# Head sums on VectorE, routing one slot earlier, and a last attention unit laid out for the experts

## The reference

```python
xn = layernorm(x)
# branch 1: linear attention, 16 heads of 32, chunks of 128, decay per head
q, k, v = silu(xn @ Wq), silu(xn @ Wk), silu(xn @ Wv)
scores  = (q @ k.T) * D                      # within a chunk
o       = scores @ v + (q @ S) * q_decay     # S: state before the chunk
S       = exp(ld * 128) * S + (k * k_decay).T @ v
o  = o * sigmoid((xn @ Wg1) @ Wg2)
o  = o * rsqrt(mean(o * o over the head's 32) + 1e-5) * norm_w
a  = o @ Wo
# branch 2: 8 experts, best 2 per token, at most 1280 slots an expert, in order of tokens
p, e = top2(softmax(xn @ Wg))
m  = sum over 2 of p * (relu(xn @ w1[e]) @ w2[e])     # 512 -> 2048 -> 512
return x + a + m
```

## Time and profile before

| what | us |
|---|---|
| median of 3 runs (2173.14 to 2176.17) | 2175.56 |
| the profiled execution | 2182.53 |
| its span, first to last instruction | 2180.8 |
| TensorE busy | 2110.3 |
| VectorE busy | 765.1 |
| ScalarE busy | 573.5 |
| GpSimd busy | 477.6 |
| mean granted TensorE clock | 0.988 of full |

### The profile page before, as it was taken

The page is one execution under the profiler, slowest core; times in us unless marked ns, Lnnn a source line. Parts: engine busy times, 40 slices in busy tenths (PEclk is TensorE's granted clock), DMA queues, the critical chain, the costliest instruction groups (busy, mean ns, idle before and its releaser), DMA issues.

```text
span 2180.8 us, 28220 instructions
## 1 busy us (share of the span) xinstructions
PE 2110.3 (97%) x11672; PEld 1741.4 (80%) x11672; DVE 765.1 (35%) x1486; ACT 573.5 (26%) x1017; POOL 477.6 (22%) x372
## 2 busy tenths in 40 slices
PE   6899999999979999999999999999999999999997
PEld 4787788778768888878887887888888888878886
DVE  5555565555454113312422322331232124223311
ACT  5222322332233212312312321231232123113211
POOL 2524442443350111020211202101010202111011
PEclk9899999999989999999999999999999999999998
DMA  4220212011025122321622413332141215224021
GB/s 151 77 78 31 70 60 78 21 60 60 32 68 198 26 49 67 118 44 44 159 28 62 111 60 68 74 111 30 52 113 59 40 49 144 42 55 112 28 30 20
DMA packets 83964, 151.39 MB, mean 69 GB/s; under 512 B 16768, under 2 KB 16768, under 8 KB 83824
## 3 DMA queue, kind: packets, MB, share of 16 engines
q1 hardware_dynamic: 63424, 105.65, 14.6%
q0 software_dynamic: 20400, 43.74, 11.4%
HBM read 109.82 MB, written 39.53 MB: 68 GB/s over the span
## 4 chain that ended last, share of the span: by engine, by line
PE 86%; DMA 5%; DVE 3%; issue 2%; POOL 2%; ACT 1%; SPq 0%; POOLq 0%; ACTq 0%; DVEq 0%
PE bank L1074 43%; PE bank L1349 29%; PE bank L1211 4%; DMA out_rows<-y,add_row 4%; PE bank L1081 3%; PE bank L1387 2%; POOL out_rows L564 1%; PE bank L1158 1%; DMA gathered<-xn_rows,gather_row 1%; PE bank L1175 1%; PE bank L1200 1%; DVE xnT_lo L801 1%; PE bank L1122 1%; PE bank L1194 1%; PE bank L1168 0%
## 5 line engine op out<-in xcount | busy, mean ns | idle before, releaser
L1026 DVE SCALAR_TENSOR_TENSOR h_lo<-bank,h_hi 128x512 fp32r<-128x512 f32 x256 | 177.1, 692 | 788.2 <-ACT h_hi L741 788.2
L1074 PE MATMUL bank<-xT_hi,w_hi 128*128 128x512 f32 x1024 | 406.6, 397 | 0.5 <-issue 0.5
L1074 PE MATMUL bank<-xT_hi,w_lo 128*128 128x512 f32 x1024 | 399.6, 390 | 0.0
L1349 PE MATMUL bank<-w_hi,h_lo 128*128 128x512 f32 x1024 | 398.6, 389 | 0.0
L1074 PE MATMUL bank<-xT_lo,w_hi 128*128 128x512 f32 x1024 | 398.5, 389 | 0.0
L1349 PE MATMUL bank<-w_hi,h_hi 128*128 128x512 f32 x1024 | 398.3, 389 | 0.0
L1349 PE MATMUL bank<-w_lo,h_hi 128*128 128x512 f32 x1024 | 398.3, 389 | 0.0
L741 ACT ACTIVATE h_hi<-bank 128x512 fp32r<-128x512 f32 x256 | 153.1, 598 | 823.5 <-PE bank L1074 823.5
L564 POOL DMA_INDIRECT out_rows<-y,add_row x80 | 128.8, 1611 | 777.0 <-ACT y L734 704.9
L1074 PEld LDWEIGHTS bank<-xT_hi,w_lo 128*128 128x128 f32 x1024 | 192.2, 188 | 41.6
L1349 PEld LDWEIGHTS bank<-w_lo,h_hi 128*128 128x128 f32 x1024 | 192.2, 188 | 39.9
(11 more groups left out here) (185 smaller groups left out, 2434.8 us busy)
## 6 DMA issues: line engine op xcount, KB each, us to landing
raw_weights<-in_L_ffn_w SPq DMA_DIRECT2D x256, 256.0 KB, 4.1
x_in<-in_L_attn_x SPq DMA_DIRECT2D x32, 256.0 KB, 3.2
xn_rows<-xn SPq DMA_DIRECT2D x32, 256.0 KB, 2.2
x_res<-in_L_attn_x SPq DMA_DIRECT2D x32, 256.0 KB, 4.6
out_rows<-y_attn SPq DMA_DIRECT2D x32, 256.0 KB, 2.0
gathered<-xn_rows,gather_row POOLq DMA_INDIRECT x80, 3.5
out_rows<-y,add_row POOLq DMA_INDIRECT x80, 5.1
attn_raw<-in_L_attn_Wq SPq DMA_DIRECT2D x4, 256.0 KB, 7.8
```

Of the source, the lines that this page charges most:

```text
L1026: v_.scalar_tensor_tensor(h_lo[f % 2][:, 0:n * P], h_bank[f % 2][:, 0:n * P], 0.0, h_hi[f % 2][:, 0:n * P].bitcast(F32), ALU.max, ALU.subt ...
L1074: last = mm(dest, at(left[l], t), at_r(right[r], t), start=(i == 0), stop=(i == n - 1))
L1349: last = mm(y_bank[i][:, :], hx[f % 2][:, part], wx[c][:, f % FPC, :], start=(f == 0 and l == 0), stop=(f == FT - 1 and l == 2))
```

## The change

**Head sums and scales.** gate_output is followed by a VectorE transposition of gated in blocks of 32x32, into a new tile turned: a head's 32 rows become 32 neighbouring columns. ScalarE squares turned, VectorE reduces over 32 columns (sum_sq), adds eps, GpSimd takes the power, VectorE multiplies turned by the scales, read with a repeated column, and transposes the product back into normed. sum_squares, turn_scales, spread_scales, head_cols and the bank for scales are gone. xn is turned into sc[0], sc[1] and the two banks of q and k.

**Routing.** turn_logits follows the four v projections, read_logits and choose follow the fourth unit's normalise (for the first group, they stand ahead of the first unit), count and read_counts are at i = 0, give_slots between that unit's masks and states, the eight route DMAs at i = 0, with the second norm_scale behind them.

**The last unit and memory.** raw lies elsewhere, so the first eight weight units are loaded at unit 28 and four are split there, four in unit 30; gather_rows(0) is in unit 29. The first four gathers are issued in unit 30, into the expert's tile y. The last unit is written out for TensorE: parts of the group's out projection stand between its steps, and the rest (finish_out) behind the first up of expert 0. Up now waits for a chunk's first four weight units only, down for all eight.

**Between experts.** The confirm of the last spare moves behind the first two gathers of the next expert.

Declarations and places of tiles, and those changes of counts that follow from the rest, are left out:

```diff
...
+                    if g == SUPERS - 1:
+
+                        sp.wait_ge(S["xn_turned"], TILES)
+                        for s in xn_stored:
+                            sp.wait_ge(s, 16 * SUPERS)
+                        for n in range(UNITS):
+                            load_unit(0, n)
                     if g > 0:
                         for j in range(TPG):
                             store_y(TPG * (g - 1) + j)
+                    if g == SUPERS - 1:
+                        sp.wait_ge(S["routed"], 16 * TOP * TILES)
+                        sp.dma_start(slot_rec[:, main_cols, :], main_slots[0]).then_inc(S["rec_loaded"], 16)
+                        sp.dma_start(slot_rec[:, spare_cols, :], spare_slots[0]).then_inc(S["rec_loaded"], 16)
...
+            def first_gathers():
+
+                pool.wait_ge(S["gather_rows_ready"], 1)
+                for s in xn_stored:
...
+                for i in range(BLOCKS[0]):
+                    pool.indirect_dma_start(y[:, i, :], None, xn_dram[:, :],
...
             for u in range(ATTN_UNITS):
                 g, i = u // GROUPS, u % GROUPS
                 if u > 0:
                     head_scales(u - 1)
-                if i == 2:
+                if i == 0:
                     for t in range(2):
                         for r in range(TOP):
                             route(g, t, r)
                 if u < ATTN_UNITS - 1:
                     decayed_k(u + 1)
                     decayed_q(u + 1)
-                if i == 2:
+                if i == 0:
                     for t in range(2, TPG):
                         for r in range(TOP):
                             route(g, t, r)
-                if i == 0 and g < SUPERS - 1:
-                    norm_scale(2 * (g + 1) + 1)
+                    if g < SUPERS - 1:
+                        norm_scale(2 * (g + 1) + 1)
                 if i == GROUPS - 1 and g < SUPERS - 2:
                     norm_scale(2 * (g + 2))
+                if u == ATTN_UNITS - 2:
+                    first_gathers()
...
                 for j in range(LAST):
                     scatter(e, j)
-                    confirm(e, j)
+                    if j < LAST - 1:
+                        confirm(e, j)
                 if e < EXPERTS - 1:
                     pool.wait_ge(S["gather_rows_ready"], e + 2)
-                    gather(e + 1, 0)
+                    gather(e + 1, 0, (0, 1))
+                confirm(e, LAST - 1)
+                if e < EXPERTS - 1:
+                    gather(e + 1, 0, (2, 3))
                 scatter(e, LAST)
                 confirm(e, LAST)
...
             def split_high(e, u):
                 act.wait_ge(raw_loaded[u % UNITS], 16 * (FPC * e + u // UNITS + 1))
                 if e == 0 and u == 0:
-                    act.wait_ge(S["k_projected"], ATTN_UNITS)
+                    act.wait_ge(S["v_projected"], TILES)
+                if e == 0 and u == FPC:
+                    act.wait_ge(S["q_projected"], ATTN_UNITS)
...
             def square(u):
-                act.wait_ge(S["gated_ready"], u + 1)
-                a.activation(squares[:, :], gated[:, :], ACT.Square).then_inc(S["squared"], 1)
-
-            def spread_scales(u):
-
-                act.wait_ge(S["head_scale_ready"], u + 1)
-                a.copy(squares[:, :].rearrange("p (c e) -> p c e", e=HD),
-                       head_scale[:, :, :].rearrange("p c h -> p (c h)").unsqueeze(2).to_broadcast([P, TPG * HPG, HD])
-                       ).then_inc(S["scale_spread"], 1)
+                act.wait_ge(S["gated_turned"], u + 1)
+                a.activation(squares[:, :], turned[:, :], ACT.Square).then_inc(S["squared"], 1)
...
-                if u > 0:
-                    spread_scales(u - 1)
-                if u < ATTN_UNITS - 1:
                     silu_k(u + 1)
                 if i == 2 and g < SUPERS - 1:
                     for j in range(TPG):
                         xnT_high(TPG * (g + 1) + j)
                 if u > 0:
                     oT_high(u - 1)
-                square(u)
+                if u < ATTN_UNITS - 1:
+                    square(u)
                 if i == GROUPS - 1 and g < SUPERS - 1:
...
-                if u >= ATTN_UNITS - 2:
-                    for r in range(4):
-                        split_high(0, 4 * (u - ATTN_UNITS + 2) + r)
+                if u == ATTN_UNITS - GROUPS:
+                    for n in range(FPC):
+                        split_high(0, n)
+                if u == ATTN_UNITS - 2:
+                    for n in range(FPC, UNITS):
+                        split_high(0, n)
             turned_high(0, 0, 0)
-            turned_high(1, 0, 1)
-            spread_scales(ATTN_UNITS - 1)
+            square(ATTN_UNITS - 1)
+            for i in range(1, BLOCKS[0]):
+                turned_high(i, 0, i)
             oT_high(ATTN_UNITS - 1)
-            turned_high(2, 0, 2)
-            turned_high(3, 0, 3)
...
-                                 ALU.mult, ALU.add).then_inc(S["mean_sq_ready"], 1)
+
+                dve.wait_ge(S["squared"], u + 1)
+                step(v_.tensor_reduce(sum_sq[:, :], squares[:, :].rearrange("p (b e) -> p b e", e=HD), AX.X, ALU.add))
+                v_.tensor_scalar(mean_sq[:, :], sum_sq[:, :], 1.0 / (4 * HD), EPS, ALU.mult, ALU.add).then_inc(S["mean_sq_ready"], 1)
...
                 v_.scalar_tensor_tensor(gated[:, :], tanh_g[:, :], 1.0, o_bank[:, :], ALU.add, ALU.mult).then_inc(S["gated_ready"], 1)
+                dve.wait_ge(S["gated_ready"], u + 1)
+                v_.transpose(turned[:, :], gated[:, :]).then_inc(S["gated_turned"], 1)
 
             def scale_heads(u):
-                dve.wait_ge(S["scale_turned"], u + 1)
-                v_.tensor_tensor(normed[:, :], gated[:, :], scale_bank[:, :], ALU.mult).then_inc(S["normed_ready"], 1)
+
+                dve.wait_ge(S["head_scale_ready"], u + 1)
+                step(v_.tensor_tensor(squares[:, :].rearrange("p (b e) -> p b e", e=HD),
+                                      turned[:, :].rearrange("p (b e) -> p b e", e=HD),
+                                      head_scale[:, :].unsqueeze(2).to_broadcast([P, TPG * HPG, HD]), ALU.mult))
+                v_.transpose(normed[:, :], squares[:, :]).then_inc(S["normed_ready"], 1)
...
+            read_logits(0)
+            choose(0)
+
             for u in range(ATTN_UNITS):
                 g, i = u // GROUPS, u % GROUPS
                 mask(u, (0, 1))
+                if i == 0:
+                    read_counts(g)
                 if u > 0:
                     mean_square(u - 1)
+                mask(u, (2, 3))
                 if i == 0:
-                    read_logits(g)
-                if i == 1:
-                    read_counts(g)
-                mask(u, (2, 3))
+                    give_slots(g)
+                    if g == SUPERS - 1:
+
+                        v_.tensor_scalar(spare_used[:, 0, :], taken[0:1, :], float(MAIN), None, ALU.is_gt)
+                        v_.tensor_scalar(spare_used[:, 1, :], taken[0:1, :], float(MAIN + P), None, ALU.is_gt).then_inc(S["spare_known"], 1)
...
-                if u == ATTN_UNITS - 2:
-                    for n in range(4):
+                    read_logits(g + 1)
+                    choose(g + 1)
+                if u == ATTN_UNITS - GROUPS:
+                    for n in range(FPC):
                         split_low(0, n)
-
-            gather_rows(0)
+                if u == ATTN_UNITS - 3:
+                    gather_rows(0)
+
+            turned_low(0, 0, 0)
             mean_square(ATTN_UNITS - 1)
-            for n in range(4, UNITS):
+            turned_low(1, 0, 1)
+            for n in range(FPC, UNITS):
                 split_low(0, n)
-            turned_low(0, 0, 0)
-            turned_low(1, 0, 1)
+            turned_low(2, 0, 2)
+            turned_low(3, 0, 3)
             scale_heads(ATTN_UNITS - 1)
             oT_low(ATTN_UNITS - 1)
-            turned_low(2, 0, 2)
-            turned_low(3, 0, 3)
...
-                wait(pe, ("masked", HPG * u), ("normed_ready", u - 1))
+                wait(pe, ("masked", HPG * u))
                 if u % GROUPS == GROUPS - 1 and u < ATTN_UNITS - 1:
-                    wait(pe, ("xnT_lo_made", TPG * (u // GROUPS + 1) + TPG - 1))
+                    pe.wait_ge(S["xnT_lo_made"], TPG * (u // GROUPS + 1) + 2)
...
-                if u % GROUPS == GROUPS - 1 and u < ATTN_UNITS - 1:
-                    pe.wait_ge(S["xnT_lo_made"], TPG * (u // GROUPS + 2))
                 turn(t_bank, kdT, TPG).then_inc(S["kd_turned"], 1)
-
-            def sum_squares(u):
-                pe.wait_ge(S["squared"], u + 1)
-                for c in range(TPG):
-                    first = SUMS.start + c * HPG
-                    last = mm(o_bank[:, first:first + HPG], squares[:, c * P:(c + 1) * P], head_cols[:, :], start=True, stop=True)
-                last.then_inc(S["summed"], 1)
-
-            def turn_scales(u):
-
```

(75 more changed lines are left out.)

108 lines of the change are left out of this document (42 added, 66 removed).

## The result

| what | us |
|---|---|
| kernel before, median of 4 runs (2173.1 to 2176.17) | 2174.35 |
| changed kernel, median of 4 runs (2135.27 to 2137.0) | 2135.66 |
| its profiled execution, and the span of that | 2135.27, 2133.5 |
| TensorE, VectorE, ScalarE, GpSimd busy | 2061.2, 826.1, 549.3, 481.7 |
| mean granted TensorE clock | 0.991 |

The ratio is 0.9823 [0.9806, 0.984]: 38.7 us faster. The forecast was 2128.5, in a range of 2102 to 2155.

The account below looks back on a forecast made before the run. TensorE, busy 97% of 2180.8 us, was taken as the bound. Gains of 26.7, 3.1, 12 and 8.3, less 4, plus 1, make 47: 2182.5 becomes 2135.5, less 7.0 from profile to median, 2128.5 us, range 2102 to 2155.

Parts of the forecast that it names:

- Part 1 and 2: Attention units: head sums leaving TensorE save 6.9 us a group; VectorE's added operations cost 1.1 us in fourth units.
- Part 3: Routing's new place: TensorE stands 1.35 us at count per group, GpSimd's routes hidden; net gain 4.45 us a group.
- The spell at 473.53: Short half-clock stretch in a fourth unit of the kernel before; it may go, 1 us.
- The sum: Whole span's gain: 26.7 + 3.1 + 12 + 8.3 - 4 = 46.1, with the half-clock spell 47 us.
- the cover of the power: GpSimd's power for the scales, 2934 ns, has some 5 us before VectorE's second multiplication wants it.
- Part 4: First group: choose ahead of the first mask leaves TensorE idle at count; 4 us lost, bounds 2 gained to 10 lost.
- Part 5: Last attention unit, last score to first down product: 12 us gained, bounds 5 to 16, 2.7 taken off for half clock.
- Part 6: Changes of expert: TensorE's five waits for gathered rows go, 8.3 us gained, bounds 4 and 8.3.
- A: Everything hidden: no new stalls, no half clock in the first group or last unit; 2105 us; chance 0.14.
- B: Every attention group: new stalls at count and in the fourth unit bring half clock, 18 us; 2147 us; chance 0.14.
- C: Transpositions make VectorE the bound in 24 units without out projection; over 2.0 us each slower, 2198 us; chance 0.04.
- D: Gathers still late, last unit still bound by its scales chain: 8 and 7 us less; 2144 us; chance 0.10.

Follow-up runs that it names:

- second chip: The changed kernel, unaltered, run again on another chip: 2136.52 us, ratio 0.9785 to the kernel before.
- the late first group: The changed kernel with only group 0 routed in its old place, its routes in one piece: 2131.25 us, ratio 0.9777.
- curing the multiplication alone: Changed kernel with groups 0 to 6 routed in the old place, GpSimd holding kdT and qdT until VectorE has multiplied: 2144.43 us, ratio 0.9836.
- the cut routes: Changed kernel with groups 0 to 6 routed in the old place, four route DMAs ending the second unit, four the third: 2137.41 us, ratio 0.9792.

## Why the prediction was right, and where it was not

**Part 1 and 2.** Confirmed in size: 711 and 671 ns for an assumed 690. Plain units pay nothing, and the fourth unit's wait at the update is 0.58 us (0.76 in every second group, some 0.5 predicted); the second wait that was priced there, 0.6 us at attend, never came. What the text gave as slack, 0.7 us in plain units, is at least that. It had no cost in the first unit for more of VectorE's time. With the hold before gate_output there are 0.56 us, and 0.8 more for another transposition; without the hold (second chip) there are none. And the 1193 ns of oT_lo in the earlier trace rows, taken as a bound for a transposition, were no duration of such an operation. In each of the first seven groups of the kernel before, one oT_lo takes 0.98 to 1.19 us, each time beside qdT:

```profile
468.70 1.27 POOL L480 TENSOR_TENSOR qdT<-qT,q_decay 128x512 f32<-128x512 f32 x1 [0.44 <-PE bank L1200]
469.32 1.19 DVE L910 TENSOR_TENSOR oT_lo<-normed,oT_hi 128x512 fp32r<-128x512 f32 x1 [0.69 <-ACT oT_hi L660]
```

So the collision stood in the trace before, and was read as the length of an operation.

**Part 3.** The wait at count is 1.36 us (1.35). A group gained 5.0 us (4.45). That is near by terms that offset each other: 7.5 us of work and waits went (6.9), the fourth unit paid 0.58 (1.1), the first 0.56 at the residuals (nothing). On the second chip, without those 0.56, a group takes 69.8 us. From the start of group 1 to the last score the kernel took 496.5 us and takes 465.35: 31.2, predicted 30.8 (26.7, 3.1 and the spell at 473.53, which went). The spell is luck: on the second chip the same kernel had two others, 2.7 and 2.9 us.

The reason given for the place of the routes was thin, though. The text counted them as hidden and took the new place as a cost of 1.35 us. The runs show that this place is a condition of part 1: with the routes where they had been, the head sums make the kernel 6 us slower (1.0028). The step that would have found this is the cover of the power, "some 5 us", which was read for units without routes ahead of it, and never for the fourth unit of the kernel before, whose power stands behind the routes of the third. What the text said of the transposed product, that it costs what its rows cost, holds only while GpSimd has no tensor operation at that time. The sum was right because the change moved both, and the text did not know that it had to.

**Part 4.** Takes came at 56.85 (55), attend of unit 1 at 84.72 (82), group 1 starts 4.3 us later (4 lost), of which 1.5 are there at the first score already. The clock in 50 to 100 us is 0.80 as before, not under it, and in 0 to 50 us it is 0.93 instead of 1.00. The run with the late first group shows that this loss is due to routing ahead of the first unit.

**Part 5.** Gained 12.7 us (12). By its steps, from the start of score: update at 5.3 (5.0), the scales at 10.0 (9.6), the hold for oT_lo 1.66 (1.8), first up 20.5 (19.8), finish_out 23.2 (22.6), first down 30.3 (28.4, with 2.7 taken off for half clock). There was no half clock; a wait of 1.44 for h_lo and 0.7 us of lateness at first up, which the text did not have, stand in its place, so that the total came out well by luck. Three of the gaps foreseen are there: 1.93, 1.66 and 0.82.

**Part 6.** 7.7 us (8.3), and 7.7 to 9.7 when undone; on the second chip the same stretch of the changed kernel is 2.0 us longer.

**The sum** was 47 from span to span, and is 47.3. **The time** was 7.2 us off, and this is one step, the last: "the median of the runs is 7.0 us below the profiled one", taken over to the changed kernel. Its profiled execution (2135.27) lies at its median (2135.66). The kernel before has medians of 2174.35, 2180.05, 2183.14 and 2179.83 us on four occasions, and its profiled 2182.53 is like those of the other chips: the three runs shown were low, or the profile was high. Which of the two, nothing here tells. On the second chip the change gains 46.6 us.

**The rivals.** A (all hidden) fell by the waits for takes and kd. B (half clock from the pair of waits) fell in size, not in kind: in the profile that was forecast all stretches of 50 us from 100 to 550 us are at 1.00. But in other profiles of the same attention half clock does follow the wait at count: in two of seven groups on the second chip, in two with the confirm put back, in one with the last unit re-ordered, 2.4 to 2.9 us each. So in some groups the wait costs this, and never in all; what decides it, no run here tells. C fell at 0.71 us a transposition. It had the right place in mind though, VectorE, and the wrong operation: with the routes in their old place a late power and one multiplication of 3.01 us a group take the whole gain of the head sums; curing the multiplication alone gave 15 us back. D fell by the missing wait for gathered rows.

## What to carry to other kernels

An edit that takes work from the bounding engine is worth what the helper's queue allows, so price the latency of the new chain through every engine it crosses, in each kind of unit, with what stands ahead of it in each queue: here a 2.9 us power behind eight DMA issues turned a gain of 20 us into a loss of 6. Parts of a change that look separate can be conditions of one another; run each alone before crediting it. When a cure brings the time that was hoped for, look whether the thing cured is gone: the cut routes gave 25 us, and the collision stood one unit earlier. And make the sum from span to span, then compare it with the difference of medians: a profile 7 us off its median is not an offset that the next kernel inherits.
